# A fused attention and ternary feed-forward kernel: ternary weights rounded by ACT and cast by DMA, token work spread over ten tiles, the transition reordered

## What is computed

```python
def xattn(q, latent_kv, Wq, Wkv_expand, Wout):      # 16 heads of 16
    ...
    scores = jnp.where(causal, q_heads @ k_heads / 4, min)
    return (softmax(scores) @ v_heads) @ Wout.T

def linear_bit(x, w, g):
    xq = act_quant(rmsnorm(x, g))                   # 8 bits, a scale per row
    s = jnp.mean(jnp.abs(w))
    wq = jnp.round(jnp.tanh(w / (s + 1e-8))) * jnp.arctanh(s)
    return jnp.einsum('bsd,od->bso', xq, wq)

x = x + xattn(layernorm(x), ctx, Wq, Wkv_expand, Wout)
z = layernorm(x)
h = silu(linear_bit(z, w1, g1)) * linear_bit(z, w2, g2)   # hidden width 1024
return x + linear_bit(h, w3, g3)
```

## Time and profile before

| what | us |
|---|---|
| median of 3 runs | 202.84 |
| lowest, highest | 201.66, 203.04 |
| the profiled execution | 202.36 |
| its span, first to last instruction | 200.6 |

### The profile page before, as it was taken

How to read it: one execution, slowest core, us unless ns; L and a number is a source line. 1 busy time by engine, 2 the same in 40 slices (tenths; PEclk the granted TensorE clock), 3 DMA queues, 4 the chain that set the end, 5 groups by cost and what they waited for, 6 DMA issues and landing times.

```text
span 200.6 us, 3287 instructions
## 1 busy us (share of the span) xinstructions
PE 148.5 (74%) x1082; PEld 97.3 (49%) x1082; DVE 164.4 (82%) x309; ACT 142.9 (71%) x195; POOL 130.0 (65%) x212
## 2 busy tenths in 40 slices
PE   5979886888779499697789764284888778775380
PEld 5567655676566377475557341131353243332360
DVE  1179799999788947999959598985989999999950
ACT  2026978985699586895769976696799998896220
POOL 4063727279885883877625669879878988997100
PEclk9999999999969958999699998557699999999588
DMA  5999920000000000000000000220234635534311
GB/s 167 320 379 423 400 117 0 7 0 0 3 2 0 3 0 0 3 0 0 0 3 2 0 0 0 52 52 5 52 80 88 149 82 115 120 78 100 83 54 54
DMA packets 20944, 15.02 MB, mean 75 GB/s; under 512 B 15296, under 2 KB 19648, under 8 KB 20416
## 3 DMA queue, kind: packets, MB, share of 16 engines
q1 hardware_dynamic: 20704, 14.42, 24.9%
q10 hardware_dynamic: 224, 0.39, 0.6%
HBM read 9.04 MB, written 2.10 MB: 56 GB/s over the span
## 4 chain that ended last, share of the span: by engine, by line
DVE 41%; POOL 15%; ACT 14%; PE 14%; issue 12%; DMA 2%; DVEq 0%; POOLq 0%; ACTq 0%
DVE c_max L1160 7%; DVE hh L1136 7%; ACT q_x L812 5%; ACT probs L769 4%; POOL u L434 4%; DVE u_max L1041 4%; PE bank L580 3%; POOL half_sum L404 3%; DVE hT L1147 3%; DVE row_max L962 3%; DVE y L1187 3%; DVE row_sum L975 2%; ACT probsT L754 2%; PE wide L587 2%; DMA out<-y 2%
## 5 line engine op out<-in xcount | busy, mean ns | idle before, releaser
L685 PE MATMUL wide<-wT,xqT 128*128 128x512 bf16 x128 | 36.0, 428 | 7.9 <-DVE hh L1136 6.7
L456 POOL TENSOR_TENSOR c_h<-hh,g3b 128x1024 f32<-128x1024 f32 x15 | 35.4, 2361 | 3.4 <-DVE hh L1136 3.3
L404 POOL TENSOR_TENSOR half_sum<-probs 128x512 f32<-128x512 f32 x16 | 20.3, 1270 | 24.9 <-ACT probs L769 24.9
L685 PEld LDWEIGHTS wide<-wT,xqT 128*128 128x128 bf16 x128 | 12.7, 107 | 25.8 <-issue 9.5
L705 PE MATMUL bank<-wT,hT 128*128 128x256 bf16 x112 | 15.9, 289 | 10.4 <-DVE hT L1147 10.4
L580 PE MATMUL bank<-woutT,attnT 128*128 128x256 f32 x64 | 20.0, 466 | 4.2 <-DVE attnT L983 4.2
L885 ACT ACTIVATE sq_junk<-hh,root_x 128x1024 bf16<-128x1024 f32 x16 | 18.3, 1147 | 5.3 <-DVE hh L1136 4.6
L769 ACT ACTIVATE probs<-probs,ln_rstd 128x1024 f32<-128x1024 f32 x16 | 18.4, 1152 | 4.9 <-DVE probs L968 4.8
L812 ACT ACTIVATE q_x<-u,round_c,qs_x 128x256 f32<-128x256 f32 x32 | 16.6, 588 | 7.1 <-issue 3.6
L434 POOL TENSOR_TENSOR u<-xc,g 128x512 f32<-128x512 f32 x16 | 20.0, 1272 | 2.4 <-ACT q_x L812 2.4
L968 DVE TENSOR_TENSOR probs<-wide,row_max 128x1024 f32<-128x1024 f32 x16 | 19.3, 1217 | 1.7 <-PE bank L506 1.6
(11 more groups left out here) (122 smaller groups left out, 303.3 us busy)
## 6 DMA issues: line engine op xcount, KB each, us to landing
out<-y SPq DMA_DIRECT2D x16, 128.0 KB, 2.0
x_sb<-in_x SPq DMA_DIRECT2D x1, 1280.0 KB, 10.3
xT<-in_xT SPq DMA_DIRECT2D x1, 1280.0 KB, 17.5
w_in<-in_w1T SPq DMA_DIRECT2D x1, 1024.0 KB, 12.3
w_in<-in_w2T SPq DMA_DIRECT2D x1, 1024.0 KB, 11.4
w_in<-in_w3T SPq DMA_DIRECT2D x1, 1024.0 KB, 13.5
x_sb<-in_x SPq DMA_DIRECT2D x1, 512.0 KB, 6.4
xT<-in_xT SPq DMA_DIRECT2D x1, 512.0 KB, 7.2
```

The source lines that it names most:

```text
L404: last = g.tensor_tensor(out=half_sum[:, t, :, :], in0=e[:, :, 0, :], in1=e[:, :, 1, :], op=ALU.add)
L456: g.tensor_tensor(out=c_h[:, t, :], in0=hh[:, t, :], in1=g3b[:], op=ALU.mult).then_inc(c_ready, 1)
L685: last = nc.tensor.matmul(wide[:, (w * 2 + n) * 512:(w * 2 + n + 1) * 512], xqT_cols(T, w * DC + c), w_cols[:, c, n * 512:(n + 1) * 512], ...
```

## The change

- **Ternary weights.** ACT's tanh writes int16 into a tile `tern`, which is q_h (unused until the FFN); the conversion rounds. A DMA issued from POOL's queue casts it to bf16 into wT. Tanh i+1 waits for DMA i, since there is one buffer. ACT runs tanh 0, 1, 2 in its iterations 3, 4, 5, right behind `recip_T_copy` and ahead of `quantise`; POOL issues the DMAs in its iterations 4, 5, 6, behind `keys`. DVE's three rounding passes go. PE waits for the three DMAs ahead of the FFN.
- **The scalar branch.** The Ln takes the place of the first tanh. POOL's series stands behind `scaled` in iterations 2 and 3, the log branch behind `scaled` in iteration 4.
- **Attention order.** PE projects ahead of `tokens_T`. DVE's two maxima of batch 1 come ahead of `sums(0)`; in its iteration 6 `divide(6)` comes behind `measure_sum(5)` and `token_max(4)`.
- **Token work.** u is scaled tile by tile. Batches 5, 6 and 7 take three FFN tiles each: `tokens_of(T)` gives the batch and the step. POOL and DVE do them in tiles 1 to 9; ACT quantises batch a in tile 3, 6 or 9 ahead of the next tile's silu; PE transposes in tiles 1, 4, 7 and 10. `dequant` is called for batches 4 and 5, and 6 and 7, together.
- **Transition.** PE and ACT take the first `up`, silu and gating between the last transposes; `quantise(4)` comes behind silu of tile 1; tile 0 has no slot of its own any more on ACT, DVE and PE, and `hidden_max(0, 0)` and `residual(7)` stand in slot 1.

```diff
+        FIRST = 5
+        def tokens_of(T):
+            return FIRST + (T - 1) // 3, (T - 1) % 3
...
+        tern = q_h[:].rearrange("p t n -> p (t n)")
...
+                def ternary(i):
+                    need(pool, tanh_ready, i + 1)
+                    g.dma_start(wT[:, i * WN:(i + 1) * WN], tern).then_inc(tern_ready[i], 16)
...
+                def scaled_tile(b, t):
+                    need(pool, xc_ready, b + 1)
+                    need(pool, qx_ready, 2 * b - 1 + t)
...
                     if live(j + 2):
                         keys(j + 2)
+                    if 0 <= j - 4 < 3:
+                        ternary(j - 4)
                     if from_(j, 2):
                         scaled(j - 2)
+                    if j == 2:
+                        series((11, 9, 7, 5))
+                    if j == 3:
+                        series((3, 1))
+                    if j == 4:
+                        log_branch()
...
                 def slot(T, t, b):
+                    a, step_ = tokens_of(T)
...
+                    if T > 0 and a < B:
+                        if step_ == 0 and a > FIRST:
+                            factor(a)
+                        if step_ < 2:
+                            scaled_tile(a, step_)
+                        else:
+                            token_scale(a)
...
                     if j == 0:
                         values_of(6, bank5)
+                    if from_(j, 1):
+                        project(j - 1)
                     if from_(j, 3):
                         need(pe, rT_ready, j)
                         tokens_T(j - 3, bank5)
-                    if from_(j, 1):
-                        project(j - 1)
...
+                probs_T(7, 0)
                 need(pe, shifted, 2 * B)
                 up(0, 0, 0, 0)
-                up(0, 0, 0, 1)
-                probs_T(7, 0)
                 project(6)
                 probs_T(7, 1)
-                up(1, 1, 0, 0)
+                up(0, 0, 0, 1)
                 weigh(7)
                 recip_T(7)
-                tokens_T(4, bank7)
-                slot(0, 0, 0)
+                up(1, 1, 0, 0)
+                up(1, 1, 0, 1)
                 project(7)
-                tokens_T(5, bank7)
-                need(pe, bank4_free, B)
+                up(2, 0, 1, 0)
                 schedule(slot)
...
-                    a.activation(w_in[:, bass.ds(i * WN, WN)], w_in[:, bass.ds(i * WN, WN)], ACT.Tanh,
+                    if i > 0:
+                        act.wait_ge(tern_ready[i - 1], 16)
+                    a.activation(tern, w_in[:, bass.ds(i * WN, WN)], ACT.Tanh,
...
                         recip_T_copy(j - 1)
+                    if 0 <= j - 3 < 3:
+                        weight_tanh(j - 3)
                     if from_(j, 3):
                         quantise(j - 3)
...
+                    a, step_ = tokens_of(T)
+                    if step_ == 0 and a - 1 < B:
+                        tokens_T_copy(a - 1, hT_banks[a % 2])
+                    if step_ == 2 and a < B:
+                        quantise(a)
...
+                probs_T_copy(7, 0)
                 silu(0, 0, 0)
-                probs_T_copy(7, 0)
                 probs_T_copy(7, 1)
+                recip_widen(7)
+                square(0, 0, 0)
+                recip_T_copy(7)
+                silu(1, 1, 0)
                 quantise(4)
...
-                def ternary(i):
-                    need(dve, tanh_ready, i + 1)
-                    v.tensor_scalar(wT[:, i * WN:(i + 1) * WN], w_in[:, i * WN:(i + 1) * WN],
-                                    ROUND, ROUND, ALU.add, ALU.subtract).then_inc(tern_ready, 1)
```

More of the change, by code:

```diff
@@ L145, in build_program @@
         ln_in, ln_out, ath_steps, ath_ready = map(sem, ("ln_in", "ln_out", "ath_steps", "ath_ready"))
-        tanh_ready, tern_ready = sem("tanh_ready"), sem("tern_ready")
-        AHEAD = 6
+        tanh_ready = sem("tanh_ready")
+        tern_ready = [sem(f"tern{i}_ready") for i in (1, 2, 3)]
+        FIRST = 5
         def from_(b, first):
             return not isinstance(b, int) or b >= first
-        def late(b):
-            return isinstance(b, int) and AHEAD <= b < B
+        def tokens_of(T):
+            return FIRST + (T - 1) // 3, (T - 1) % 3
         def live(b):
@@ L235, in dequantised @@
         def dequantised(b):
-            return max(b + 1, 4)
+            return 4 if b < 4 else 6 if b < 6 else 8
         def last_tile(T):
@@ L378, in arctanh_terms, with series @@
                     step(g.tensor_tensor(out=sq, in0=w_s[:], in1=w_s[:], op=ALU.mult))
-                    step(g.tensor_scalar(poly, sq, 2.0 / 13, 2.0 / 11, ALU.mult, ALU.add))
-                    for n in (9, 7, 5, 3, 1):
+                def series(terms):
+                    for n in terms:
+                        if n == 11:
+                            step(g.tensor_scalar(poly, sq, 2.0 / 13, 2.0 / 11, ALU.mult, ALU.add))
+                            continue
                         step(g.tensor_tensor(out=poly, in0=poly, in1=sq, op=ALU.mult))
                         step(g.tensor_scalar(poly, poly, 2.0 / n, None, ALU.add))
-                    step(g.tensor_tensor(out=poly, in0=poly, in1=w_s[:], op=ALU.mult))
+                        if n == 1:
+                            step(g.tensor_tensor(out=poly, in0=poly, in1=w_s[:], op=ALU.mult))
+                def ternary(i):
+                    need(pool, tanh_ready, i + 1)
+                    g.dma_start(wT[:, i * WN:(i + 1) * WN], tern).then_inc(tern_ready[i], 16)
                 def log_branch():
@@ L428, in token_scale @@
                     last.then_inc(qsx_ready, 1)
+                def scaled_tile(b, t):
+                    need(pool, xc_ready, b + 1)
+                    need(pool, qx_ready, 2 * b - 1 + t)
+                    g.tensor_tensor(out=u[:, t, :, :], in0=xc[:, t, :].unsqueeze(1).to_broadcast([P, 2, D]),
+                                    in1=g12[:], op=ALU.mult).then_inc(u_ready, 1)
                 def scaled(b):
-                    need(pool, xc_ready, b + 1)
-                    need(pool, qx_ready, 2 * b)
                     for t in range(TB):
[L434 to L437, removed]
+                        scaled_tile(b, t)
                 def iteration(j):
@@ L488, in _ @@
                 iteration(1)
[L489 to L493, removed]
+                log_inputs()
+                for j in range(2, B - 1):
                     iteration(j)
@@ L668, in _ @@
                     iteration(j)
-                pe.wait_ge(tern_ready, 3)
+                for i in range(3):
+                    pe.wait_ge(tern_ready[i], 16)
                 def xqT_cols(T, n):
@@ L700, in down @@
                         need(pe, lastT_ready, T + 1 - LAST)
-                    if T == 1:
-                        pe.wait_ge(xqT_ready, AHEAD)
+                    if T == 0:
+                        need(pe, bank4_free, B)
                     need(pe, y_ready, T - 1)
@@ L806, in quantise @@
                 def quantise(b):
-                    need(act, u_ready, b + 1)
+                    need(act, u_ready, 2 * b + 2)
                     need(act, qsx_ready, b + 1)
@@ L857, in _ @@
                 recip_T_copy(1)
-                act.wait_ge(inv_ready, 1)
-                weight_tanh(0)
+                act.wait_ge(ln_in, 1)
+                a.activation(w_ln[:], w_ln[:], ACT.Ln).then_inc(ln_out, 1)
                 recip_widen(2)
@@ L866, in _ @@
                 query_copy(4)
[L867 to L873, removed]
+                act.wait_ge(inv_ready, 1)
+                for j in range(3, B - 2):
+                    iteration(j)
                 def silu(T, t, b):
@@ L1039, in token_max @@
                 def token_max(b):
[L1040 removed]
+                    need(dve, u_ready, 2 * b + 2)
                     v.tensor_reduce(out=u_max[:, bass.ds(b * 2 * TB, 2 * TB)].rearrange("p (t w) -> p t w", w=2), in_=u[:],
@@ L1111, in _ @@
                     aggregate(b)
-                sums(0)
                 maximum(1, 0)
                 maximum(1, 1)
+                sums(0)
                 shift(1, 0)
@@ L1119, in _ @@
                     aggregate(b)
[L1120 to L1127, removed]
+                for j in range(1, B - 2):
+                    iteration(j)
                 dve.wait_ge(w_down_ready, 2)
@@ L1206, in slot @@
                         hidden_worth(T - 1, 1 - t)
-                    if front:
+                    if step_ == 2 and a < B:
                         token_max(a)
                         token_recip(a)
-                    if measured:
+                    if step_ == 0 and FIRST < a < B:
+                        need(dve, bank4_free, a + 1)
                         measure_sum(a)
```

53 lines of the change are left out of this document (15 added, 38 removed).

## The result

The kernel after took 207.68 us (median of 4 runs, 206.28 to 210.9), the kernel before 202.55 beside it: ratio 1.024 with the 95% interval 1.014 to 1.033. Ratios leave out runs that fell in a slower state of the chip, here the one of 210.9. It is slower, by some 5 to 7 us. The profiled execution took 206.28 us, its span is 204.5.

What follows compares the result with a forecast made beforehand. DVE was busiest (164.4 of 200.6 us) but not full, held up by waits on POOL, ACT and PE. Last exponential 5.3 us later, tiles and tail even: span 205.9, plus 1.76 is 207.7, stated as 207.6; range 201.0 to 212.0.

Steps and rivals of the forecast that it cites:

- The wait: ACT ahead of the second and third tanh, iterations 4 and 5: stands about 6.5 us each for the cast DMA.
- L: Time from POOL's turn for the cast DMA to its landing, issue included: taken as 3.7 us.
- Iterations 2 and 3: Attention iterations: periods of 10.82 and 11.0 us, against 12.18 and 12.8 before.
- Sums(4): Start of DVE's row sum that opens attention iteration 4: expected at 62.8, 4.0 us ahead of before.
- The wait for u: DVE in iteration 2: its 1.36 us wait goes, as seven of twelve POOL series steps stand behind u.
- Before iteration 2: Two maxima of batch 1 fill DVE's 1.19 us wait for POOL: 0.85 us gained, row sum at 40.95.
- Iterations 4 and 5: Attention periods of 14.4 + L, 18.1 us each, plus 1.5 for dequantisation in the second; iteration 6 starts at 100.5.
- Row sum of iteration 6 to the last exponential: End of the attention part: stays 10.6 us, gain and loss within 1, so the last exponential ends at 111.1.
- The tiles: FFN, last exponential of batch 7 to gating of tile 15: 77.9 us as before, with POOL waits of about 2.0.
- The tail: Span behind the gating of the last tile: 16.9 us before, taken as even.
- the full pay of the spread: Rival, FFN tiles 1 to 10: POOL's waits go, tiles run at DVE's rate, -6.7 us; 199.7 us, chance 0.13.
- The slow cast: Rival, iterations 4 and 5: cast DMA lands like the 512 KB load, 6.4 us; 213.0 us, chance 0.12.

Runs made afterwards that it cites:

- e1: Kernel after with three int16 buffers, so that no tanh waits for a DMA: 194.72 us, ratio 0.970 to the kernel before.
- e2: Kernel after with one buffer kept and POOL issuing each cast DMA one iteration earlier, behind u: 195.87 us, ratio 0.967 to the kernel before.
- e4: Kernel after with the cast DMA issued at the head of the same POOL iteration, ahead of the token scale: 200.58 us, ratio 1.002 to the kernel before.
- e7: e2 plus a one-column Exp on ACT behind the copies that follow the Ln, to load the table early: 192.67 us, ratio 0.961 to the kernel before.
- e9: The kernel before, unchanged, measured once more as if it were an experiment: 201.96 us, ratio 1.010 to the kernel before.
- e10: Attention part of the kernel after with transition and FFN slots of the kernel before: 207.29 us, ratio 1.033 to the kernel before.
- e5: Attention part of the kernel before with transition and FFN slots of the kernel after: 202.68 us, ratio 1.015 to the kernel before.
- e11: The kernel after, unchanged, measured again: 207.26 us, ratio 1.033 to the kernel before.
- e6: e2 with ACT quantising batches 5, 6 and 7 a tile later, behind silu and square: 189.56 us, ratio 0.946 to the kernel before.
- e3: Kernel after with tanh in place in fp32 and the three rounding passes back on DVE: 197.85 us, ratio 0.987 to the kernel before.

## Why the prediction was right

The forecast, 207.6 us, stands beside 207.68, which is closer than the working deserves: terms that were off by about 1 us balanced. The forecast was for an execution like the profiled one, and that took 206.28; its span, 204.5, is 1.4 under the 205.9 of the sum. The median reached the forecast because other runs were slower, which nothing in the sum foresaw.

- *The wait* was told with its place and its size: ACT stands behind the DMA in iterations 4 and 5, about 6.5 us each; the rows show 6.41 and 5.61. e1 shows that it is the cost, e2 and e4 that POOL's queue (3.2 us expected and measured, and 0.2 more from the row sum to its start) and the landing make it up. L was taken as 3.7 from the transposes and measured 3.05 to 3.16, which is 1.2 us too much in two iterations. The row of 3.1 for half the bytes was nearer than that row plus 0.6.
- *Iterations 2 and 3.* Sums(4) came at 64.04, not 62.8. The step that failed: "The Ln takes the place of the first tanh, and its return load falls before an Exp that waits for DVE, so the 1.28 us leave the path." The row shows the load starting at 46.50, after 2.39 us of idle ended by DVE: it stands behind the Exp's wait, not ahead of it. The wait for u went as forecast, but DVE then waited 1.24 us for the half sum at 52.32. By e7 the load cost 1.2 us over iterations 2 and 3, the whole of the miss here: without it the periods are 10.8 and 11.1, where 10.8 and 11.0 were forecast.
- *Before iteration 2:* 40.89 against 40.95.
- *Iterations 4 and 5:* 17.9 and 19.1, expected 18.1 and 19.6. In iteration 4 the three terms measured 3.4 (row sum to issue), 3.16 and 11.3 us (tanh to next row sum) for 3.2, 3.7 and 11.2.
- *Row sum of iteration 6 to the last exponential:* 10.2, expected 10.6. E, the end of that exponential, was expected at 111.1 and came at 111.2: 1.2 late at sums(4), then 0.2 and 0.5 short in the two periods and 0.4 short here.
- *The tiles:* 77.9 expected, 78.0 measured, with the three waits of POOL of 2.05 us where 2.0 were expected. The old order has 77.8 to 77.9 in three profiles (before, e9, e10), the new one 78.0 to 78.8 in the kernel after, e5 and e11, and e6 shows that those waits are what keeps the spread from paying.
- *The tail* was taken as even; it was 1.6 us shorter in this profile. The last y waits for a store for 0.98 us here and 2.95 before. In e9, the kernel before once more, it waits 0.97, and in e4, whose order at the end is that of the kernel after, 3.22. So it differs between executions and is no effect of the change. First e9, then e4:

```profile
196.63 0.48 DVE L1187 SCALAR_TENSOR_TENSOR y<-bank,dq_h,x_sb 128x256 f32<-128x256 f32 x1 [0.97 <-DMA out<-y]
```

```profile
196.69 0.48 DVE L1194 SCALAR_TENSOR_TENSOR y<-bank,dq_h,x_sb 128x256 f32<-128x256 f32 x1 [3.22 <-DMA out<-y]
```

Of the rivals, the full pay of the spread needed ACT's order changed; e6 did just that and got some 4 of the 6.7 us. The slow cast did not come: three landings of 3.0 to 3.1 us in the kernel after, and 4.0 at the most in e4.

## What to carry to other kernels

A wait on a DMA lasts as long as what stands ahead of the issue in the issuing engine's queue, plus the landing, less what the waiting engine still has to do, and it delays all that stands behind it there; look for the issue's place before the transfer's length. One buffer was enough once the DMA was issued in the iteration that produced the data. Work that is spread to level one engine pays only if no other engine's order makes that engine wait again at the seams.

## What the runs showed of the hardware that was not expected

The Exp table load of 1.28 us runs behind the semaphore wait of the Exp that needs it, so idle ahead of that wait does not hide it (46.50 in the kernel after); a small Exp ahead of the wait moves it, to 43.53 in e7. The casting DMA of 512 KB takes 0.64 to 0.80 us of POOL and lands in 3.0 to 3.1 in the kernel after, no later than a transpose of half the bytes; in e4 two of three took 3.6 and 4.0. A POOL instruction on 128x2 elements, run beside a rounding pass of DVE, took 1.46 us for two in place of 0.59 (e3 against the kernel after). The eight matmuls of a projection took 1.99 us at a granted clock of 1.00 and 3.65 at 0.53, in kernels with the same attention order (e2, e1). Taking the rounding off DVE saved 2.3 us where its three passes take 3.6 (e3 against e1).
